# Perceiver block: key projections of a half spread over twelve steps in place of ten, and each step's weighing put into the next step

## What is computed

```
q = (layernorm(x) @ Wq)   # 32 heads of 16
k = (ctx @ Wk)            # 8 heads of 16, each used by 4 query heads
v = (ctx @ Wv)
probs = softmax(q @ k.T * 16 ** -0.5)
x = x + (probs @ v) @ Wo
```

## Time and profile before

| | |
|---|---|
| median of 3 runs | 4295.67 us (4290.4 to 4313.48) |
| the profiled execution: own time, and span from first to last instruction | 4310.48 us, 4308.7 us |
| TensorE busy in the span | 3636.9 us (84%) |
| busy VectorE, ScalarE, GpSimd | 2328.9, 1356.4, 1396.8 us |
| mean granted TensorE clock | 0.93 of 2.4 GHz |
| the 416 steps | from 116.19 to 1049.28 us |
| in 116 to 1000 us (884 us) | TensorE busy 844.89, VectorE 522.50, ScalarE 497.75, GpSimd 364.61 us, clock 0.97 |

### The profile page before, as it was taken

The page is one execution under the profiler, slowest core; times in us unless marked ns, Lnnn a source line. Parts: engine busy times, 40 slices in busy tenths (PEclk is TensorE's granted clock), DMA queues, the critical chain, the costliest instruction groups (busy, mean ns, idle before and its releaser), DMA issues. The chain is left out here.

```text
span 4308.7 us, 72516 instructions
## 1 busy us (share of the span) xinstructions
PE 3636.9 (84%) x31360; PEld 2407.9 (56%) x31360; DVE 2328.9 (54%) x2671; ACT 1356.4 (31%) x1764; POOL 1396.8 (32%) x892
## 2 busy tenths in 40 slices
PE   6999999996566469999999999999999989575678
PEld 3566666663222345777777777777777744322224
DVE  3666556553399652444444444444444325598972
ACT  1555555554243011222222222222222102344430
POOL 4344444440098110111111111111111002496970
PEclk8999999997689789999999999999999999687999
DMA  6455455442221032111111111111111210221211
GB/s 187 123 143 137 136 142 139 135 125 37 52 81 62 20 129 79 37 35 37 37 35 40 32 44 37 37 44 37 44 37 40 79 64 3 67 81 56 79 51 37
DMA packets 216517, 303.62 MB, mean 70 GB/s; under 512 B 64856, under 2 KB 161688, under 8 KB 214792
## 3 DMA queue, kind: packets, MB, share of 16 engines
q1 hardware_dynamic: 216200, 299.00, 23.8%
HBM read 245.38 MB, written 53.10 MB: 69 GB/s over the span
## 5 line engine op out<-in xcount | busy, mean ns | idle before, releaser
L1336 POOL TENSOR_TENSOR D_ctx_lo<-D_ctx_raw,D_ctx_hi 128x1904 fp32r<-128x1904 f32 x64 | 255.6, 3994 | 1386.5 <-ACT D_ctx_hi L1330 1386.5
L580 DVE TENSOR_REDUCE A_mxc<-A_psX 128x2 f32<-128x768 f32 (+2 forms) x512 | 489.4, 990 | 267.2 <-PE A_psX L610 264.9
L800 ACT ACTIVATE A_probs<-A_psE 128x1024 f32<-128x1024 f32 (+1 forms) x416 | 426.5, 1025 | 329.4 <-PE A_psE L824 323.4
L1354 ACT ACTIVATE D_V<-D_psY 119x384 f32<-119x384 f32 x224 | 110.1, 491 | 957.8 <-PE D_psY L1421 957.8
L1370 DVE TENSOR_REDUCE D_mxc<-D_psE 128x4 f32<-128x1904 f32 (+1 forms) x128 | 242.4, 1894 | 259.1 <-PE D_psE L1440 258.9
L234 POOL TENSOR_TENSOR ES_dBx<-E_du,E_Bn 128x512 f32<-128x512 f32 x256 | 317.6, 1281 | 70.9 <-POOLq L49 69.0
L1652 ACT ACTIVATE D_probs<-D_psE 119x2048 f32<-119x2048 f32 x112 | 210.6, 1880 | 406.2 <-PE D_psE L1773 406.2
L1787 PE MATMUL D_psO<-D_probs,D_V 119*32 119x256 f32 (+1 forms) x5376 | 331.0, 397 | 0.0
L1697 DVE TENSOR_TENSOR D_acc<-D_acc,D_probs 119x1024 f32<-119x1024 f32 x96 | 117.7, 1226 | 379.9 <-ACT D_probs L1652 379.9
L1421 PE MATMUL D_psY<-D_wv_hi,D_ctx_hi 128*119 128x384 f32 (+1 forms) x896 | 313.5, 350 | 7.5 <-ACT D_V L1354 6.6
L1421 PE MATMUL D_psY<-D_wv_hi,D_ctx_lo 128*119 128x384 f32 (+1 forms) x896 | 302.2, 337 | 0.0
(11 more groups left out here) (310 smaller groups left out, 7393.3 us busy)
## 6 DMA issues: line engine op xcount, KB each, us to landing
D_ctx_raw<-in_ctx SPq DMA_DIRECT2D x48, 952.0 KB, 5.2
A_land<-in_ctx SPq DMA_DIRECT2D x32, 768.0 KB, 5.3
A_land<-in_ctx SPq DMA_DIRECT2D x16, 1024.0 KB, 5.5
E_Bn<-bc_scratch SPq DMA_DIRECT2D x64, 256.0 KB, 3.6
E_Cn<-bc_scratch SPq DMA_DIRECT2D x64, 256.0 KB, 3.4
k_scratch<-A_Khl SPq DMA_DIRECT2D x32, 384.0 KB, 5.5
A_Kst<-k_scratch SPq DMA_DIRECT2D x64, 192.0 KB, 3.6
A_land<-in_ctx SPq DMA_DIRECT2D x16, 642.0 KB, 4.3
```

The source lines that it names most:

```text
L580: nc.vector.tensor_reduce(mxc[:, u % 4, :, u // 4], psX[:, x % 2, :, 0:w], axis=AX_X, op=ALU.max).then_inc(x_free, 1)
L800: nc.scalar.activation(probs[0:KW[k], n % NPR, :, :].rearrange("p h q -> p (h q)"), psE[0:KW[k], :], ACT.Exp, scale=HD ** -0.5).then_inc(e ...
L1336: nc.gpsimd.tensor_tensor(ctx_lo[c][:, :, 0:w], ctx_raw[c][:, :, 0:w], ctx_hi[c][:, :, 0:w].bitcast(F32), ALU.subtract).then_inc(lo_done[c ...
```

## The change

Two edits. Before, each of chunks 1 and 3 of the keys was projected in two steps with six passes each, and half 0 had no projection in k = 10, 11 and 12; now each chunk takes three steps with four passes each, up to k = 11. Before, TensorE weighed in odd steps only, the two steps before (a step alone at the start of a batch); now each step n weighs step n-1.

```
-    K_STEPS = [(0, 3), (3, 2), (5, 3), (8, 2)]
+    K_STEPS = [(0, 3), (3, 3), (6, 3), (9, 3)]
...
-                            if n and n % STEPS == 0:
-                                weigh(n - 1)
-                            elif n % 2:
-                                if n % STEPS > 1:
-                                    weigh(n - 2)
+                            if n:
                                 weigh(n - 1)
```

## The result

The median fell from 4296.04 us (5 runs, 4290.4 to 4313.48) to 4276.56 us (5 runs, 4273.32 to 4280.63): ratio 0.9945, 95% interval 0.9922 to 0.9968, so 24 us faster by the ratio, 19.5 by the medians. The sum of the forecast was 34.2; the median lies 0.6 us above the forecast's own range of 4250 to 4276, and within the range with its rivals, 4248 to 4290. The two profiled executions took 4310.48 and 4280.63 us.

A forecast was written before the change was run, and what follows sets the result against it. TensorE's order plus its waits, chiefly for ScalarE's exponential, was taken to bound the steps. Terms -8.7 (order), -22.0 (clock) and -3.5 (last batch) sum to -34.2 from the median 4295.67: 4262 us, own range 4250 to 4276.

The forecast's parts named there:

- its rivals: The first rival and a dear weighing alone (4279 us, chance 0.07) widen the range to 4248 to 4290.
- The order of TensorE in a batch: Fifteen projecting batches: single weighings and four-pass projections give -0.58 us per batch, -8.7 in all; bounds -28 to +9.
- steps 9 to 12: From the projection in 9 to the scores of 13: 6.43 us become 6.55, starting 0.44 earlier, so -0.32.
- Steps 0 and 1: Start of a batch: claimed to stay as they are, no change in time.
- Steps 2 to 8 and 13 to 25: Split weighings: -0.02 us in 2 to 8, with six passes fewer, and -0.24 in 13 to 25.
- the shortest distance of two scores: Between scores of successive steps: 1.69 us claimed as the least possible, one exponential lying between.
- The last batch: Batch without projection, at low clock: every step takes 1.98 us, saving 0.58 for each of six pairs, -3.5.
- The wait of L824: Scores waiting for exponential L800 in the steps: from 46 to about 25 us, half of that in the last batch.
- The key chunks: Chunk 3 complete some 4 us later, covered by 9.5 us; 3.2 us more slack before unit 12; costs nothing.
- The slower rival: Stacked keys come late, holding up the queue, unit 12 and TensorE: 4320 us, chance 0.05.
- The clock: Half-clock falls in steps 10 to 13 of four batch pairs vanish as gaps close: -22.0 us, bounds 0 and 22.
- The first rival: The clock keeps falling, its falls hanging on something other than these gaps: 4284 us, chance 0.24.

The follow-up runs named there:

- Experiments 3: Against the kernel before, only the weighing of each step moved into the next one, key projections left at ten steps; 4285.22 us, ratio 0.9968.
- experiment 5: Against the changed kernel, single weighings only where a step would else be too short and in the last batch, pairs elsewhere; 4263.27 us, ratio 0.9922 to before.
- experiments 2: Against the kernel before, only the key projections spread over twelve steps, weighing still in pairs; 4286.31 us, ratio 0.9978.
- the filled kernel: Order of before with matmuls nobody reads put into TensorE's waits of steps 10 and 12; 4290.75 us, ratio 0.9991.
- experiment 7: The kernel before, unedited, one more profiled execution; 4287.9 us, no lengthened batch (none partly at half clock), steps end at 1029.09.
- experiment 6: Against the kernel before, key projections done in eight steps, two each, meant to lengthen the waits; 4303.49 us, ratio 1.0018.
- 8: The filled kernel, unedited, one more profiled execution; 4288.11 us, no lengthened batch, steps end at 1028.19.
- 4: Against the kernel before, matmuls nobody reads fill TensorE's waits after the scores of steps 10 and 12; 4290.75 us, ratio 0.9991.

## Why the prediction was right, and which term was mis-sized

*The order of TensorE in a batch* (forecast -0.58, to 56.7 us): 57.32 to 56.69, -0.63 or -9.4 in fifteen. Its mechanism held: the weighing alone kept its price in an even step too (0.56 in step 10), steps 10 and 11 have no wait, and two waits stay, at steps 12 and 25. Experiments 3 and 5 measured the split at 0.12 and 0.11 us, where the rows of a pair and of a weighing alone had given 0.11. That the sum came out within 0.05 is in part luck. Measured from scores to scores, as means over the batches at full clock, steps 9 to 12 gave -0.48 where -0.32 was forecast: step 11 takes 2.18 us (254.85 to 257.03) and not the 2.36 of my sum, for its four passes cost 0.70 (255.84 to 256.54) ahead of `max_rows`, not the 0.79 that they cost ahead of scores, and `max_rows` behind them 0.49, not 0.60. Steps 0 and 1, which I had staying, cost 0.08 more. Steps 2 to 8 and 13 to 25 came to +0.02 and -0.26, for -0.02 and -0.24. The 1.69 us that I called the shortest distance of two scores is not that: my own row of step 18 has 1.58 with a wait in it. No term rests on it.

*The last batch* (forecast -3.5): 50.05 to 46.98, -3.1; experiments 2 and 3 show it to be the weighing's alone. The wait of L824 came down to 11.8 us, not to the 25 that I had expected. I had taken the whole wait of the last batch as staying, and the weighings fill about half of it (10.7 before, 5.6 now); in the other batches the two waits that stay are 0.21 each, not 0.35.

*The key chunks* (forecast 0, and 3.2 us of slack): in batch 2 the queue of the changed kernel stores chunk 3 at 265.10, after a split done at 258.64, so 6.5 us of cover are left of 9.5; the read-back lies at 268.70, and unit 12 at 277.95. SyncE's queue, GpSimd and TensorE:

```profile
265.10 0.53 SPq L530 DMA_DIRECT2D k_scratch<-A_Khl  x1
268.70 2.47 SPq L536 DMA_DIRECT2D A_Kst<-k_scratch  x4
```

```profile
257.77 0.87 POOL L557 TENSOR_TENSOR A_Khl<-A_Kf,A_Khl 128x321 fp32r<-128x321 f32 x1
```

```profile
277.95 0.42 PE L610 MATMUL A_psX<-A_Kst,A_Qst 50*128 50x322 f32 x2
```

With 3.6 us to land the keys are there at 274.8, 3.2 before their use. The slower rival did not come about.

*The clock* (forecast -22.0) is the term that was mis-sized. It is right for the execution it was read from: all eight lengthened batches are gone, and the three terms together give the measured 34.3 at the end of the steps. But I subtracted it from the median, with the sentence that the falls should stand in every execution: that step failed. Another execution of before has two such batches, another none, and there the steps end near 1029 to 1030 us, as they do with the waits filled. The average is what counts: 6 us by the filled kernel, and by the two comparisons of before and after what the order leaves, 19.5 - 12.5 = 7 and 22.7 - 12.5 = 10. The same subtraction leaves 2.5, 6.4 and 2.3 us in experiments 2, 3 and 5. So by the medians the average gain in clock lies between 2 and 10 us (by the ratios between 1 and 11), and is not known more closely. The forecast had its clue on the page: the profiled execution was 14.8 us slower than the median, and I put that down to other layers. By the three profiles of before it lay in the steps: in the first these ended 19 to 20 us later than in the other two, and the layers behind them took 3259 us against 3259 and 3257. Read as falls that the median doesn't have, it would have left 7 of the 22, and the sum would have been 4276. That the steps ended 34.3 us sooner, as summed, hangs on the execution of before: against that of experiment 7 it would have been 14.

*The first rival*, that the clock keeps falling, gave 4284 and is wrong in its mechanism. In either profile of the changed kernel only the first 5 us of batch 0 and, as before, the second half of the last batch ran at half clock. But its time lies 7.4 from the median, the forecast's 14.6. The Trainium skill ("TensorE: Matmul & The Clock Gate", section "HAM oscillation — how this bites in real kernels") looks for the cause of falls in long waits for a transfer. In batches 1 to 14 here the clock fell with no wait of TensorE over 1.2 us, and none of these waits was for a transfer; the measurement differs from what that section describes.

What brings the falls is open in part. Profiles with both waits as in before (before three times, experiment 6) have 8, 2, 0 and 1 lengthened batches of 15 each. Those in which at least one of the two was shortened or filled (the changed kernel twice, experiments 2 to 5 and 8) have none in seven times 15. All falls that lengthened batches 1 to 14 begin in step 11 or 13, behind these waits (batch 0 begins at the low clock in every kernel). So the waits are needed, as far as these runs go; whether longer ones bring more was not tested, and what decides in which execution and batch one leads to a fall was not found. The spread of the timed runs is no sure sign either: 11, 7 and 11 us over the twelve runs each of experiments 2 to 4, 32 over the 47 of before, but 5 in experiment 6, which has both waits. Also open are the 1 to 4 us by which the changed kernel does better than its order and the filled kernel's gain explain. Two small parts of them can be seen: 0.5 us behind the last exponential, at whose end a pair of weighings was still running before, and up to 1.4 us in the last batch, which took 51.40 us in one execution of before.

## What to carry to other kernels

Before a gain in clock is subtracted from a median, count the falls in more than one execution, and ask what a distance between the profiled time and the median consists of: here, by three profiles, it held the very falls that I credited. Small groups of matmuls of another shape cost their entry and exit each time, 0.11 to 0.12 us here, so split them only in the steps that are too short for the exponential: that brought the end of the steps another 13.7 us forward. A forecast of TensorE's order from distances between starts in one batch held to 0.05 us in its sum and to 0.16 in its parts; four passes cost 0.70 us ahead of one kind of work and 0.79 ahead of another. And when an edit is meant to lengthen a wait, read that wait in the new trace before the result is taken as a test: in experiment 6 it had not moved.

## What the hardware showed that I had not expected

Half-clock stretches of 3.4 and 10.2 us in the midst of the steps, the longer one after 3.4 us in which TensorE was busy for 65%, in one execution in eight batches, in another in two, in a third in none, for the same instructions and the same waits. And the kernel of experiment 6, with the same two waits and 0.54 us of another, had a narrower spread, 4301.27 to 4306.51 over twelve runs, than the kernel before on the same chip with 4287.18 to 4314.37 over 17.
